# An earlier load of x tile 3, convolution 5 behind gate product 4, and a new order on ScalarE in the head of a one-core FFN kernel

## The reference

```python
agg_w = sum_k att[b, k] * weight[k]            # 128 x 128
y  = agg_w @ x[b] + agg_b[b]                   # convolution, then bf16
qg, sg = quant(y * inv_gate);  qu, su = quant(y * inv_up)    # row-wise to integers in -127..127
gate = (qg @ w_gate.T) * sg * s_wgate          # 2048 -> 1024
up   = (qu @ w_up.T)   * su * s_wup            # 2048 -> 1024
inter = clip(silu(gate) * up, -10, 10)         # bf16
qi, si = quant(inter * inv_inter)
out[b] = x[b] + (qi @ w_down.T) * si * s_wdown # 1024 -> 2048
```

## Time and profile before

| what | value |
|---|---|
| median of 3 runs | 831.01 us (830.33 to 831.53) |
| the profiled execution, its own time | 831.8 us |
| its span in the trace | 830.0 us |
| mean granted TensorE clock | 0.992 |
| TensorE busy | 802.8 us (97%) |
| VectorE busy | 715.8 us (86%) |
| ScalarE busy | 441.4 us (53%) |
| GpSimd busy | 143.5 us (17%) |

### The profile page before, as it was taken

How to read it: one execution, slowest core, us unless ns; L and a number is a source line. 1 busy time by engine, 2 the same in 40 slices (tenths; PEclk the granted TensorE clock), 3 DMA queues, 4 the chain that set the end, 5 groups by cost and what they waited for, 6 DMA issues and landing times.

```text
span 830.0 us, 9248 instructions
## 1 busy us (share of the span) xinstructions
PE 802.8 (97%) x3556; PEld 368.9 (44%) x3556; DVE 715.8 (86%) x810; ACT 441.4 (53%) x385; POOL 143.5 (17%) x136
## 2 busy tenths in 40 slices
PE   7789896999999999999999999999999999999997
PEld 4434442444444444444444444444444444444443
DVE  6955789699888889988888998888899888888968
ACT  5666223555566555456654545655454566545441
POOL 1600050222012222201222220122222102222000
PEclk9989998999999999999999999999999999999999
DMA  9972724465444545445355444435545444554332
GB/s 297 241 155 51 152 101 151 140 148 158 118 142 121 166 148 156 140 121 146 115 165 159 145 141 126 146 108 165 164 141 140 138 140 107 162 164 140 94 111 101
DMA packets 158340, 118.76 MB, mean 143 GB/s; under 512 B 147540, under 2 KB 147668, under 8 KB 148823
## 3 DMA queue, kind: packets, MB, share of 16 engines
q1 hardware_dynamic: 156568, 105.59, 42.3%
q0 software_dynamic: 1728, 12.58, 7.4%
HBM read 60.48 MB, written 33.55 MB: 113 GB/s over the span
## 4 chain that ended last, share of the span: by engine, by line
PE 88%; DMA 5%; DVE 4%; ACT 2%; issue 1%; DVEq 0%; ACTq 0%
PE gate_ps L564 26%; PE up_ps L564 25%; PE down_ps L644 23%; PE conv_ps L510 12%; DMA xt<-x 2%; DMA wd<-w_downT 1%; DVE xt L1171 1%; DMA out<-xt 1%; PE gate_ps L644 1%; DVE down_sc L1166 1%; ACT qg L751 0%; DVE xt L1020 0%; PE conv_ps L515 0%; ACT wd L796 0%; DVE part_max L1081 0%
## 5 line engine op out<-in xcount | busy, mean ns | idle before, releaser
L644 PE MATMUL down_ps<-wd,qiT 128*128 128x512 bf16 x896 | 211.2, 379 | 0.0
L564 PE MATMUL gate_ps<-wg,qgT 128*128 128x512 bf16 x928 | 206.8, 380 | 0.0
L564 PE MATMUL up_ps<-wu,quT 128*128 128x512 bf16 x896 | 202.4, 379 | 0.0
L1002 DVE TENSOR_REDUCE amax<-region 128x1 f32<-128x2048 f32 (+1 forms) x90 | 173.0, 1923 | 1.2
L406 POOL TENSOR_TENSOR prod<-wexp,att_bc 128x1024 f32<-128x1024 f32 x28 | 53.4, 1907 | 538.4 <-DVE region L1060 527.7
L644 PEld LDWEIGHTS down_ps<-wd,qiT 128*128 128x128 bf16 x896 | 87.6, 98 | 123.3 <-issue 29.7
L564 PEld LDWEIGHTS gate_ps<-wg,qgT 128*128 128x128 bf16 x928 | 91.0, 98 | 111.3 <-issue 3.8
L564 PEld LDWEIGHTS up_ps<-wu,quT 128*128 128x128 bf16 x896 | 87.7, 98 | 105.7
L510 PE MATMUL conv_ps<-xt,aggw 128*128 128x512 f32 x244 | 118.6, 610 | 11.4 <-DMA xt<-x 10.4
L751 ACT ACTIVATE qg<-region,recip 128x2048 f16<-128x2048 f32 x30 | 60.0, 2002 | 122.0 <-DVE recip L1012 117.7
L740 ACT ACTIVATE y<-conv_ps,aggb 128x512 bf16<-128x512 f32 x118 | 80.9, 687 | 75.2 <-PE conv_ps L510 70.3
(11 more groups left out here) (162 smaller groups left out, 570.2 us busy)
## 6 DMA issues: line engine op xcount, KB each, us to landing
xt<-x SPq DMA_DIRECT2D x31, 1024.0 KB, 4.8
out<-xt SPq DMA_DIRECT2D x30, 1024.0 KB, 4.0
wg<-w_gateT POOLq DMA_DIRECT2D x4, 1024.0 KB, 19.4
wu<-w_upT POOLq DMA_DIRECT2D x4, 1024.0 KB, 16.8
wd<-w_downT POOLq DMA_DIRECT2D x4, 1024.0 KB, 8.8
invg_bc<-inv_gate SPq DMA_DIRECT2D x1, 1024.0 KB, 8.0
out<-xt SPq DMA_DIRECT2D x2, 512.0 KB, 2.7
xt<-x SPq DMA_DIRECT2D x2, 512.0 KB, 3.9
```

Source lines behind the costliest of these rows:

```text
L564: last = nc.tensor.matmul(acc[:, n * BANK:(n + 1) * BANK], codes[:, k * P:(k + 1) * P], wts[:, k, n * BANK:(n + 1) * BANK], start=(k == 0) ...
L644: last = nc.tensor.matmul(down_bank(t, c), qiT_at(t)[:, k * P:(k + 1) * P], wd[:, k, c * BANK:(c + 1) * BANK], start=(k == 0), stop=(k == ...
L1002: nc.vector.tensor_reduce(amax[:, i:i + 1], src, axis=AX.X, op=ALU.max, apply_absolute_value=True).then_inc(max_ready, 1)
```

## The change

x tile 3 is loaded when the first chunk of `w_gateT` has landed, no longer after `quant_g(1)`. For this tile 1's product moves from x slot 3 to parts 6 and 7 of `wd`, and the staged rows that stood there move to the second half of `wu`; GpSimd's loads of `w_upT` therefore wait until all rows are spread. Tile 1's up codes move to part 2 of `wd`, and the chunks of `w_downT` are loaded in the order 0, 2, 3, 1 with other waits; down 0 reads its blocks in the order 0, 1, 4 to 7, 2, 3. On TensorE `turn_g(2)` and `turn_g(3)` move ahead of `turn_u(0)` and `turn_u(1)`, and ScalarE's order follows. Down 2 uses the banks of `up_ps` and `down_ps`. Convolution 5 runs whole, behind the whole of gate 4. VectorE makes tile 4's up scale before the results of tile 2. Tile 0's expert sum has six experts on VectorE instead of five, and two of the six filler matmuls go.

```diff
--- before.py
+++ after.py
@@ -79,13 +79,13 @@
             return flat if dt == bf16 else flat.bitcast(dt)
 
         Y_HOME = [y[:, :], wd_part(0, bf16), wd_part(1, bf16)]
-        XG_HOME = [region1[:, :], xt[:, (XS - 1) * H:XS * H]]
+        XG_HOME = [region1[:, :], wd[:, :, :].rearrange("p k h -> p (k h)")[:, 6 * H:8 * H].bitcast(fp32)]
         prod_flat = prod[:, :, :].rearrange("p k o -> p (k o)")
         GATE_HOME = [down_sc2[:, :], prod_flat, region2[:, 0:I], region1[:, 0:I]]
         UP_HOME = [region2[:, I:H], y[:, :].bitcast(fp32), region2[:, I:H], region1[:, I:H]]
         QGT_HOME = [qgT[:, :], wd_part(2, bf16), wd_part(5, bf16)]
-        QUT_HOME = [wd_part(3, bf16), wd_part(4, bf16), quT[:, :], qgT[:, :]]
-        XU_HOME = wd[:, :, :].rearrange("p k h -> p (k h)")[:, 6 * H:8 * H].bitcast(fp32)
+        QUT_HOME = [wd_part(3, bf16), wd_part(2, bf16), quT[:, :], qgT[:, :]]
+        XU_HOME = XG_HOME[1]
         qg_bf = qg[:, :].bitcast(bf16)
         QIT_HOME = [qg_bf[:, 0:KI * P], qg_bf[:, KI * P:2 * KI * P]]
 
@@ -129,7 +129,7 @@
         quT16 = quT[:, :].bitcast(fp16)
         qiT16 = qiT[:, :].bitcast(fp16)
 
-        rows_s = wd[:, :, :].rearrange("p k h -> p (k h)")[:, 4 * H:8 * H].bitcast(fp32)[0:1, :]
+        rows_s = wu[:, KH // 2:KH, :].rearrange("p k i -> p (k i)").bitcast(fp32)[0:1, :]
         invi_s = wd_part(3, fp32)[0:1, :]
         swd_s = [quT[0:1, :].bitcast(fp32), qu[0:1, :].bitcast(fp32)]
 
@@ -157,7 +157,7 @@
         b2_s = qiT32[:, P + 3 * B:P + 3 * B + K]
         bk_kept = qiT32[:, P + 3 * B + K:P + 3 * B + 2 * K]
 
-        SPLIT = 5
+        SPLIT = 6
         diag_at = [region2[:, I:H], prod_flat, region2[:, I:H], prod_flat]
 
         def diag_part(t, k):
@@ -283,7 +283,8 @@
         last_turn_ps = [bank(up_ps, h).bitcast(fp16)[:, 0:BANK] for h in range(2)]
 
         EARLY_DOWN = [[bank(down_ps, 0), bank(down_ps, 1), bank(gate_ps, 0), bank(gate_ps, 1)],
-                      [bank(gate_ps, 0), bank(gate_ps, 1), bank(down_ps, 0), bank(down_ps, 1)]]
+                      [bank(gate_ps, 0), bank(gate_ps, 1), bank(down_ps, 0), bank(down_ps, 1)],
+                      [bank(up_ps, 0), bank(up_ps, 1), bank(down_ps, 0), bank(down_ps, 1)]]
 
         def gate_acc(t):
             return up_ps if t in (1, EARLY) else gate_ps
@@ -296,7 +297,7 @@
 
         def down_bank(t, c):
             if t < EARLY:
-                return EARLY_DOWN[min(t, 1)][c]
+                return EARLY_DOWN[t][c]
             return LAST_DOWN[t][c] if t >= B - 2 else bank(down_ps, c % 2)
 
         def xcols(t, c):
@@ -333,7 +334,7 @@
             for i in range(2):
                 sp.dma_start(swd_s[i], rows[:, (5 + i) * I:(6 + i) * I]).then_inc(rows_in[2 + i], 16)
             sp.dma_start(xslot(2), x[2, :, :]).then_inc(x_in[2], 16)
-            sp.wait_ge(gcodes_ready, 2)
+            sp.wait_ge(wg_in[0], 16)
             sp.dma_start(xslot(3), x[3, :, :]).then_inc(x_in[3], 16)
 
             def turn_g(t):
@@ -432,6 +433,7 @@
             for i in range(2):
                 pool.wait_ge(rows_in[2 + i], 16)
                 spread(swd_bc[:, i * I:(i + 1) * I], swd_s[i])
+            pool.wait_ge(row_spread, SWD)
             for i in range(WCH - 1):
                 load(wu, w_upT, i, wu_in)
             pool.wait_ge(wexp_in, 16)
@@ -439,15 +441,14 @@
             load(wu, w_upT, WCH - 1, wu_in)
             for i in range(1, WCH):
                 pool.wait_ge(wg_in[i], 16)
-            pool.wait_ge(row_spread, SWD)
             pool.wait_ge(xu_ready, 3)
             load(wd, w_downT, 0, wd_in)
-            pool.wait_ge(up_done, 1)
-            load(wd, w_downT, 1, wd_in)
+            pool.wait_ge(gate_done, 3)
+            load(wd, w_downT, 2, wd_in)
             pool.wait_ge(ucodes_ready, EARLY + 1)
             load(wd, w_downT, 3, wd_in)
             pool.wait_ge(up_done, 2)
-            load(wd, w_downT, 2, wd_in)
+            load(wd, w_downT, 1, wd_in)
             pool.wait_ge(prod_ready, 2)
             aggregate(4)
             aggregate(5)
@@ -574,7 +575,7 @@
                     elif t == 2 or t == EARLY:
                         pe.wait_ge(gateval_ready, t - 1)
                     elif t == EARLY + 1:
-                        pe.wait_ge(scaled_ready, NC * 2 + 2)
+                        pe.wait_ge(scaled_ready, NC + 2)
                     elif t > EARLY + 1:
                         pe.wait_ge(gateval_ready, t)
                 for k in ks:
@@ -598,6 +599,8 @@
                         pe.wait_ge(upval_ready, t - 1)
                     else:
                         pe.wait_ge(upval_ready, t)
+                        if t == EARLY + 1:
+                            pe.wait_ge(scaled_ready, NC * 2 + 2)
                 for k in ks:
                     if t == 0 and k % (KH // WCH) == 0:
                         pe.wait_ge(wu_in[k // (KH // WCH)], 16)
@@ -633,22 +636,26 @@
                     if c < 2:
                         pe.wait_ge(scaled_ready, c + 3)
                 elif t == 2:
-                    pe.wait_ge(scaled_ready, NC + c + 1)
+                    if c == 0:
+                        pe.wait_ge(upval_ready, EARLY + 1)
+                    elif c >= 2:
+                        pe.wait_ge(scaled_ready, NC + c + 1)
                 else:
                     pe.wait_ge(scaled_ready, NC * t + c - 1)
-                for k in range(KI):
+                ks = (0, 1, 4, 5, 6, 7, 2, 3) if t == 0 else range(KI)
+                for k in ks:
                     if t == 0 and c == 0 and k % (KI // WCH) == 0:
                         pe.wait_ge(wd_in[k // (KI // WCH)], 16)
                     if t == B - 1 and c == 0 and k % (KI // 2) == 0:
                         pe.wait_ge(lturn_out, k // (KI // 2) + 1)
                     last = nc.tensor.matmul(down_bank(t, c), qiT_at(t)[:, k * P:(k + 1) * P],
-                                            wd[:, k, c * BANK:(c + 1) * BANK], start=(k == 0), stop=(k == KI - 1))
+                                            wd[:, k, c * BANK:(c + 1) * BANK], start=(k == ks[0]), stop=(k == ks[-1]))
                 last.then_inc(down_done, 1)
 
             HALVES = range(KH // 2), range(KH // 2, KH)
 
             pe.wait_ge(filler_set, 1)
-            for _ in range(6):
+            for _ in range(4):
                 nc.tensor.matmul(bank(down_ps, 0), filler[:, 0:P], filler[:, P:P + BANK], start=True, stop=True)
             aggregate_mm(0)
             conv(0)
@@ -666,13 +673,13 @@
             conv(3)
             gate(0, range(8, 12))
             gate(1, range(8, 12))
+            turn_g(2)
             turn_u(0)
             gate(0, range(12, KH))
             gate(1, range(12, KH))
-            turn_g(2)
             gate(2)
+            turn_g(3)
             turn_u(1)
-            turn_g(3)
             gate(3)
             turn_u(2)
             up(0)
@@ -693,12 +700,11 @@
                 down(1, c)
             for c in range(NC):
                 down(2, c)
-            conv(5, range(2))
             for t in range(4, B):
                 gate(t, HALVES[0])
+                gate(t, HALVES[1])
                 if t == 4:
-                    conv(5, range(2, NC))
-                gate(t, HALVES[1])
+                    conv(5)
                 if t == B - 1:
                     up_by_columns(t)
                     for c in range(NC - 1):
@@ -874,16 +880,16 @@
             turned_g(1, range(1, 2))
             quant_u(0)
             conv_out(3)
-            turned_u(0)
             quant_g(2)
             turned_g(2)
+            turned_u(0)
             quant_u(1)
             silu(0)
             quant_g(3)
-            silu(1)
-            turned_u(1)
             turned_g(3)
             quant_u(2)
+            turned_u(1)
+            silu(1)
             silu(2)
             turned_u(2)
             quant_u(3)
@@ -899,9 +905,8 @@
             quant_g(4)
             fix_g(4)
             quant_u(4)
-            conv_out(5, range(2))
             fix_u(4)
-            conv_out(5, range(2, NC))
+            conv_out(5)
             quant_i(3)
             fix_i(3)
             for t in range(4, B):
@@ -1029,7 +1034,7 @@
                     dve.wait_ge(row_spread, INVU)
                     dve.wait_ge(agg_mm, 3)
                 elif t == 2:
-                    dve.wait_ge(row_spread, SWU)
+                    dve.wait_ge(gcodes_ready, 2)
                 elif t == EARLY + 1:
                     dve.wait_ge(gcodes_ready, t + 1)
                 else:
@@ -1219,10 +1224,9 @@
             quant_g(4)
             for c in range(NC):
                 result(1, c)
-            result(2, 0)
-            result(2, 1)
             quant_u(4)
-            result(2, 2)
+            for c in range(NC - 1):
+                result(2, c)
             inner_tail(3)
             for t in range(4, B):
                 result(t - 2, 3)
```

## The result

The changed kernel took 816.2 us (median of 4 executions, 814.7 to 818.8), the kernel before 830.8 on the same chip: a ratio of 0.983, 95% interval 0.980 to 0.985, so 14.6 us less. The forecast was 813.5 with a range of 811.5 to 819. In a second comparison on another chip (the first experiment) it was 817.7 against 833.6, a ratio of 0.981 (0.978 to 0.984). The profiled execution took 815.9 us, its span is 814.1 instead of 830.0.

What follows compares the result with a forecast made beforehand. TensorE's fixed work was taken to bound the kernel from 160 us on, so time won in the head is kept if VectorE follows. Terms 0.5 + 11.9 + 0.3 + 4.8 = 17.5 us gave a median of 813.5, range 811.5 to 819.

Steps and rivals of the forecast that it cites:

- 1 start: Before conv(0): fewer fillers let it start sooner, 0.5 us won, between 0.9 won and about 1.0 lost.
- 2 x 3 and codes: Conv(3) to gate 3: earlier x 3 load and tile 2 codes bring gate 3 to 58.5 from 70.38, 11.9 us won.
- 3 w_downT: Down(0,0) to conv(4): the 2.35 us wait goes but returns as some 2.2 ahead of conv(4), 0.3 us won.
- 4 convolution 5: Gate 4 to down(3,0): up 4 starts 7.2 us sooner, 2.4 bare at down(3,0), so 4.8 us won.
- the rest of the loop: TensorE's loop after down(3,0): no idle from then on, so nothing more won or lost.
- the price on swiglu(2): VectorE ahead of conv(4): swiglu(2) meets POOL's aggregation of tile 4 and is lengthened by up to 0.9 us.
- VectorE following: Behind conv(5): VectorE's 1.0 us of lateness is worked off within a round, costed at nothing, bound 1.0 lost.
- the clock's falling at the new waits: Rival at conv(4) and down(3,0): each fall costs some 1.9 us, 815.4 for one, 817.3 for both; chance 0.25.
- the case without it: Whole kernel, no clock fall at conv(4) or down(3,0): median 813.5 us, within 812.5 to 814.9; chance 0.43.
- (b): Rival at conv(3): x 3 lands no sooner, 6.5 us won there instead of 11.9, 818.9 us; chance 0.08.
- (c): Rival at conv(5): x 5's transfer holds back tile 4's up-code transposes, 2.5 to 4 us lost, 816 to 817.5; chance 0.10.
- (d): Rival in the loop: each tile from 5 on waits for its x, 835 us at 0.8 a tile; chance 0.03.

Runs made afterwards that it cites:

- the first experiment: The changed kernel run once more with no edit, beside the kernel before on another chip: 817.7 us against 833.6, ratio 0.981.
- The version with seven fillers: Changed kernel plus six fillers ahead of the expert sum, one behind, eight matmuls ahead of conv(4), tile 3's codes between conv(5)'s copies: 812.8 us, 0.976.

## Why the prediction was right, and where it was off

Against the profiled execution, 15.9 us won in the span, by the forecast's own steps:

| step | forecast | measured | from |
|---|---|---|---|
| 1 start | 0.5 | 0.67 | gate 1's half at 33.19, 33.86 before |
| 2 x 3 and codes | 11.9 | 11.87 | up 0 at 65.63, 78.17 before, less 0.67 |
| 3 w_downT | 0.3 | 0.48 | conv(4) at 104.04, 117.06 before, less 12.54 |
| clock at conv(4) | 0 | -1.42 | 104.04 to 109.46, before 117.06 to 121.06 |
| 4 convolution 5 | 4.8 | 4.65 | down(3,0) at 142.33, 158.58 before, less 11.60 |
| the rest of the loop | 0 | -0.35 | a wait of 0.3 on VectorE's down_out in the last rounds |
| sum | 17.5 | 15.90 | |

1. **Start.** Right for this execution and wrong as a dependable gain. The step named the risk of conv(0) at 1.2 GHz and took 0.5 "since the activity before conv(0) hardly changes". The runs show a toss: gate 1's half came at 35.58 to 35.67 in three experiments' traces with this start, and at 33.19 in the first, so 2.4 later. Against the 33.86 of the kernel before that is 1.7 to 1.8 lost, outside the step's bound of 1.0. Undoing the step cost nothing that four executions show, and the old start can be tossed the same way.
2. **x 3 and tile 2's codes.** Right in mechanism and size, start by start. Undone singly, the load and the order are worth 5.8 us each in the traces.
3. **w_downT.** Right: 2.35 us of wait removed, 0.5 won, and the wait stands again ahead of conv(4) with 1.93. Undone, it made no difference that the times show, and 0.67 us in the trace beside the clock. Of the price on swiglu(2) nothing is seen (1.23 us, its usual length): GpSimd began just behind it and met the residual addition instead, 1.98 against 1.34 before. In the execution where the addition came first, conv(4) started at 102.17, 15.1 behind down(0,0) instead of 16.8: 1.7 won, outside the bound of 0.8 that the step had set. The Trainium skill (SBUF — State Buffer, SBUF: two separate sides) says that a VectorE operation with two inputs from SBUF and a GpSimd operation that reads SBUF exclude each other for a whole instruction. The addition's end 0.55 us behind GpSimd's agrees; the forecast had set this against the wrong instruction.
4. **Convolution 5.** Right. Waits of 0.95, 1.06 and 2.20 stand where 1.1, 0.8 and 2.4 were forecast. That fix_i(3) stands behind conv_out(5) on ScalarE is shown by the experiment that moved the codes.
5. **VectorE following.** Right: from gate 5 on TensorE is 16.2 sooner and keeps this to within 0.35.

The failed part is the choice of the likeliest case. The forecast gave the clock's falling at the new waits 0.25 and put the number on the case without it. By the mean clocks of ten executions it fell in eight, in five of them twice. The forecast's own prices, 815.4 for one and 817.3 for both, fit the groups (816.3 and 818.4) to within 1.1, and its 1.9 for a fall stands against 1.7 in the traces. That 813.5 fits the two executions without a fall (813.6) is in part luck: they took 812.5 and 814.7, and in the one that has a profile conv(4) came 1.7 us sooner behind down(0,0) and gate 1's half 1.3 sooner than before, where the forecast had 0.3 and 0.5. The forecast had two rows beside the new waits of 2.2 and 2.4, 2.35 without and 2.52 with a fall. Over all profiles waits of 1.93 to 2.35 went both ways, and each of the seven of 2.52 or more had a fall behind it, so the new waits lay where either may happen. Rivals (b), (c) and (d) did not come about: x 3 was there in time, the up codes' transposes took 4.2 us (3.9 taken), and no wait recurs in the loop.

What stays open: why the clock rises ahead of conv(0) in some executions and behind it in others. The version with seven fillers, whose clock was up before the expert sum, has one profile and four executions. Whether the old start's low clock losses (one in four) are its shorter wait ahead of conv(4) or luck is open too.

## What to carry to other kernels

When a wait is removed, ask what the next wait in line is set by, and price the wait that comes up in its place together with the clock behind it: the 2.35 us won at down(0,0) were worth 0.5. A wait of 2 us on TensorE is not 2 us but 2 or 3.7, and matmuls on constants that end just before the data comes make it 2 again. Their bank must be free, and where the data can also come early they hold it up, here by 0.9 us; with two such waits dealt with the clock held in all 13 executions of three versions, but no gain in the median was shown for the fillers at conv(4) alone. And when a copy or a quantization holds back a later engine, look first at its place in its own engine's order: one instruction moved on ScalarE won 3.3 us by the medians, 1.3 of it in the traces without a fall.

## What the runs showed of the hardware

- The same program's executions differ in how often TensorE's clock falls. Conv(4)'s waits of 1.93, 1.95 and 2.29 had a fall behind them in three profiles, its 1.97 had none in a fourth; down(3,0)'s 2.2 had one in four profiles of eight; w_downT's 2.35 had none. All seven waits of 2.52 to 6.37 had one. Behind the first 16 us, waits of 0.2 to 1.7 never had one. One fall cost 1.5 to 1.7 us.
- The granted clock of the records reads 1.00 in executions where conv(0)'s first pair takes 3.72 to 3.75 us instead of 1.95, and over the fillers, four of which took 1.91 us, at 1.2 GHz. For the first 14 us it is the matmuls' own length that tells.
- A residual addition of 0.69 us took 0.97 to 2.33 beside GpSimd's aggregation, and a product of 2.29 took 3.24 to 4.04 beside its spreads, by which of the two instructions came first.
